# A block joins the deferred blocks, and the adapter's products take operands in high and low parts

## What is computed

```python
x = x + _L0_cond_ref(x, L0_cond_W1, L0_cond_b1, L0_cond_v, itok_B_0_2)
x = x + _L1_cond_ref(x, condB_zX[:, None], condB_zY[:, None], condB_zR[:, None], 1, 1)
x = x + _L2_cond_ref(x, itok_B_0_6, L2_cond_down_w, ..., L2_cond_ln_g, L2_cond_ln_b)
x = x + _L3_cond_ref(x, L3_cond_tau_ctx, condB_tauraws, L3_cond_Wg, ..., L3_cond_Wout, ...)

# L0: softmax-weighted sums over positions, p is 2048 x 2048 with a prefix, suffix or leave-one-out mask
pooled = jnp.einsum('bjl,bld->bjd', p, hidden) / cnt[..., None]
# L1: neighbours in the channel direction (x) and in the position direction (y), reflected at the ends
du_dt = zX[:, :, None] * lap_x + zY[:, :, None] * lap_y + zR[:, :, None] * y * (1.0 - y)
# L2: the adapter, 512 -> 128 -> 512, then a layer norm
z = jax.nn.relu(jnp.einsum('bsh,bhk->bsk', hidden, Wd) + bd)
y = hidden + jnp.einsum('bsk,bkh->bsh', z, Wu) + bu
# L3: exponential averages over positions, a gate from [x, ctx], two traces, soma, gate, output
ctx = causal_ema(x, tau_ctx)
wg = jax.nn.sigmoid(jnp.einsum('btc,ec->bte', jnp.concatenate([x, ctx], axis=-1), Wg) + bg)
```

## Time and profile before

| | us |
|---|---|
| median of 3 runs (lowest, highest) | 701.6 (700.96, 702.64) |
| the profiled execution, its own time | 702.7 |
| its span in the trace | 700.7 |
| TensorE, VectorE, ScalarE, GpSimd busy | 666.1, 526.5, 363.3, 174.2 |

### The profile page before, as it was taken

The page is one execution under the profiler, slowest core; times in us unless marked ns, Lnnn a source line. Parts: engine busy times, 40 slices in busy tenths (PEclk is TensorE's granted clock), DMA queues, the critical chain, the costliest instruction groups (busy, mean ns, idle before and its releaser), DMA issues.

```text
span 700.7 us, 8057 instructions
## 1 busy us (share of the span) xinstructions
PE 666.1 (95%) x2792; PEld 484.8 (69%) x2792; DVE 526.5 (75%) x747; ACT 363.3 (52%) x745; POOL 174.2 (25%) x259
## 2 busy tenths in 40 slices
PE   4969988989999999999999999999999999999996
PEld 1535444468577868786878687868786878687875
DVE  2676789847996888589868986887689649864955
ACT  0143366582675366536653566456635653565245
POOL 5003440110044214411451235123512210111001
PEclk9989999999999999999999999999999999999998
DMA  7996998999522661465147524742465230022001
GB/s 201 326 335 222 258 203 201 359 263 322 106 36 74 150 101 29 102 135 97 30 117 129 87 35 120 131 77 39 127 93 88 38 83 1 0 48 74 0 1 60
DMA packets 51670, 85.77 MB, mean 122 GB/s; under 512 B 8480, under 2 KB 10528, under 8 KB 51630
## 3 DMA queue, kind: packets, MB, share of 16 engines
q0 software_dynamic: 16896, 33.56, 30.1%
q1 hardware_dynamic: 31230, 51.69, 20.6%
q10 hardware_dynamic: 3504, 0.01, 0.3%
HBM read 63.22 MB, written 22.04 MB: 122 GB/s over the span
## 4 chain that ended last, share of the span: by engine, by line
PE 79%; DVE 9%; ACT 4%; DMA 4%; SPq 2%; issue 1%; POOLq 0%; ACTq 0%; POOL 0%; DVEq 0%
PE bank L1130 20%; PE bank L1129 20%; PE bank L1131 20%; PE bank L1184 3%; PE bank L1174 3%; PE bank L1125 3%; PE bank L1030 3%; DMA beside_scratch<-xts 2%; PE bank L1164 2%; PE bank L1193 2%; DMA xts<-in_xT 1%; SPq L410 1%; DVE xb L1513 1%; DVE x2b L1519 1%; PE bank L1224 1%
## 5 line engine op out<-in xcount | busy, mean ns | idle before, releaser
L1668 DVE TENSOR_TENSOR_SCAN tr<-alpha,carry,tr 128x512 f32<-128x512 f32 x48 | 58.8, 1267 | 0.0
L1129 PE MATMUL bank<-th,wg_l 128*128 128x512 f32 x128 | 52.0, 406 | 0.0
L1129 PE MATMUL bank<-xh,wg_l 128*128 128x512 f32 x128 | 51.9, 406 | 0.0
L1130 PE MATMUL bank<-tl,wg_h 128*128 128x512 f32 x128 | 50.5, 395 | 0.0
L1130 PE MATMUL bank<-xl,wg_h 128*128 128x512 f32 x128 | 50.5, 395 | 0.0
L1131 PE MATMUL bank<-th,wg_h 128*128 128x512 f32 x128 | 50.2, 392 | 0.0
L1131 PE MATMUL bank<-xh,wg_h 128*128 128x512 f32 x128 | 50.2, 392 | 0.0
L840 ACT ACTIVATE carry<-tr 128x2 f32<-128x2 f32 x32 | 6.6, 205 | 80.4 <-DVE tr L1668 80.3
L624 POOL TENSOR_TENSOR rs_a<-ss_a,consts 128x1 f32<-128x1 f32 x32 | 14.3, 447 | 118.7 <-ACT junk L788 118.1
L1125 PE MATMUL bank<-xb,probT 128*128 128x512 f32 x64 | 36.4, 652 | 5.5 <-DVE xb L1513 5.4
L1655 DVE SCALAR_TENSOR_TENSOR wgb<-wgb,soma 128x512 f32<-128x512 f32 x32 | 22.2, 692 | 25.4 <-ACT wgb L834 25.4
(11 more groups left out here) (264 smaller groups left out, 1995.3 us busy)
## 6 DMA issues: line engine op xcount, KB each, us to landing
x2b<-beside_scratch POOLq DMA_DIRECT2D x12, 1024.0 KB, 9.2
xr<-rows_scratch POOLq DMA_DIRECT2D x10, 1024.0 KB, 10.6
xb<-in_x SPq DMA_DIRECT2D x8, 1024.0 KB, 14.2
result<-xr SPq DMA_DIRECT2D x7, 1024.0 KB, 4.2
x2b<-rows_scratch POOLq DMA_DIRECT2D x6, 1024.0 KB, 9.5
x_scratch<-xb SPq DMA_DIRECT2D x5, 1024.0 KB, 10.5
beside_scratch<-xts SPq DMA_DIRECT2D x5, 1024.0 KB, 11.5
late_y<-x_scratch SPq DMA_DIRECT2D x20, 256.0 KB, 2.9
```

The costliest lines, as they stand in the source:

```text
L1129: pe.matmul(acc, wl, xh_, start=start, stop=False)
L1130: pe.matmul(acc, wh, xl_, start=False, stop=False)
L1668: ve.tensor_tensor_scan(t[:, d], alpha[:, 1 + d:2 + d].broadcast_to([P, GN]), t[:, d], 0.0 if first else carry[:, k, 1 + d:2 + d], ALU.mul ...
```

## The change

1. `HEAD_BLOCKS` is 2. Block 2 leaves `mix_local`, `channels`, `by_local` and `stencil` of the first stage. Instead SyncE copies it within SBUF (`keep_x1`), and its four tiles are worked on as deferred tiles around the start of the last stage: tiles 0 and 1 beside `x3_lo(0)`, tiles 2 and 3 inside group 0. `add_before(2)` and `add_after(2)` move to the end of group 0.
2. A deferred block is loaded in one DMA of 1 MB into its own buffer `x2_of(q)`. `late_mix` reads that buffer and writes the new single buffer `late_mixed`.
3. From block 1 on, `down` and `up` go through `split3`. ScalarE writes the high parts (`x2_evict` into fp32r, a second `relu` pass, `adapter_hi` in groups 0 and 3), VectorE the low parts (`x2_lo`, four passes; `z_low`, one; `adapter_lo` in groups 0 and 3). `x2_lo` uses `junk`, `junk_o`, `late_mixed` and `late_side` as its four buffers, `z_h` is in `late_side`.
4. In VectorE's list `trace_lo(g, k)` stands one place later, `late_stencil` of tile 3 ahead of `logits(g, 0)`, and tile 2 is handled ahead of `out_apply` 2, no longer 3.
5. The adapter's weights for batch 1 are loaded in group 3, into the same buffers as batch 0's.

```diff
-HEAD_BLOCKS = 3
+HEAD_BLOCKS = 2
...
+        x2h, x2l = wide_r[:], [t[:] for t in (junk_r, junk_o_r, late_mixed_r, late_side_r)]
+        z_h, z_l = late_side_r[:], nar_r[:]
...
+                    def keep_x1(q):
+                        sp.wait_ge(x1_done, GT * (q + 1))
+                        sp.wait_ge(beside_out[0][0], 32)
+                        sp.dma_start(x2_of(q), x1_of(q)).then_inc(late_in, 16)
+
+                    def load_late(q):
+                        sp.wait_ge(x1_out[q], 16)
+                        if q == HEAD_BLOCKS + 1:
+                            beside_landed(sp, 1, 3)
                         else:
-                            sp.wait_ge(late_v, n)
-                            sp.wait_ge(late_chan, 3 * n)
-                        sp.wait_ge(x1_out[q], 16)
-                        sp.dma_start(late_y[:], x1_rows(q)[:, c]).then_inc(late_in, 16)
+                            sp.wait_ge(x3_done, GT * (q - 1))
+                        sp.dma_start(x2_of(q), x1_rows(q)).then_inc(late_in, 16)
...
                     def late_mix(q, c):
                         n, b = late_tile(q, c), q // NG
-                        act.wait_ge(late_in, 16 * (n + 1))
-                        if q == HEAD_BLOCKS:
-                            beside_landed(act, 1, 1)
+                        act.wait_ge(late_in, 16 * (q - 1))
+                        if n:
+                            act.wait_ge(late_v, n)
                         else:
-                            act.wait_ge(x3_done, GT * (q - 1))
-                        act.activation(x2_of(q)[:, c], late_y[:], ACT.Identity, ...
+                            act.wait_ge(pool_mm, B * NT)
+                        if c == 0 and q > FIRST_LATE:
+                            act.wait_ge(down_mm, q - 1)
+                        act.activation(late_mixed[:], x2_of(q)[:, c], ACT.Identity, ...
...
+                        if q:
+                            act.activation(z_h, bank[DOWN(q)][:], ACT.Relu, ...)\
+                               .then_inc(z_act, 1)
...
                     def down(q):
...
+                        pe.wait_ge(aw_lo, 2 * (q // NG + 1))
+                        for k in ks:
+                            pe.wait_ge(x2T_lo, KE * (q - 1) + k + 1)
+                            last = split3(bank[DOWN(q)][:], dw_h[:, k], dw_l[:, k], x2h[:, k], x2l[k],
+                                          k == 0, k == KE - 1)
+                        last.then_inc(down_mm, 1)
+
+                    def up(q):
+                        pe.wait_ge(z_lo, q)
+                        for c in range(GT):
+                            split3(bank[UP(q)[c]][:], z_h[:, chunk(c)], z_l[:, chunk(c)], uw_h[:], uw_l[:],
+                                   True, True).then_inc(up_mm, 1)
...
+                    def x2_lo(q):
+                        for k in ks:
+                            ve.wait_ge(x2T_ev, KE * q + k + 1)
+                            ve.scalar_tensor_tensor(x2l[k], bank[X2T(q)[k]][:], up_cols[:, q // NG, k:k + 1],
+                                                    f32(x2h[:, k]), ALU.add, ALU.subtract).then_inc(x2T_lo, 1)
+
+                    def z_low(q):
+                        ve.wait_ge(z_act, 2 * q + 1)
+                        ve.tensor_tensor(z_l, z[:], f32(z_h), ALU.subtract).then_inc(z_lo, 1)
...
                         if g == 0 and k == 0:
-                            beside_landed(ve, 1, 3)
+                            beside_landed(ve, 1, 2)
...
                         logits(g, 1)
                         blend_traces(g, 0)
                         traces(g, 1)
-                        trace_lo(g, 0)
+                        if g == 0:
+                            late_by_local(2, 3)
+                            late_stencil(2, 3)
                         logits(g, 2)
                         blend_traces(g, 1)
+                        trace_lo(g, 0)
                         traces(g, 2)
+                        logits(g, 3)
+                        if g == 0 or g == NG - 1:
+                            adapter_lo((g + 1) // NG)
+                        blend_traces(g, 2)
                         trace_lo(g, 1)
-                        logits(g, 3)
-                        blend_traces(g, 2)
+                        if adapted:
+                            x2_lo(g + 1)
                         traces(g, 3)
                         trace_lo(g, 2)
+                        if adapted:
+                            z_low(g + 1)
                         blend_traces(g, 3)
```

More of the change, by code:

```diff
@@ L968, in _ @@
                         mod_affine(g)
+                        if g == 0:
+                            late_mix(2, 2)
                         keep_traces(g, 0)
@@ L972, in _ @@
                         trace_hi(g, 0)
+                        if g == 0:
+                            late_mix(2, 3)
                         keep_traces(g, 1)
@@ L1011, in _ @@
                         for c in range(GT):
-                            if late and c == 3:
+                            if late and c == 2:
                                 late_mix(g + 3, 2)
```

151 lines of the change are left out of this document (91 added, 60 removed).

## The result

| | before | changed |
|---|---|---|
| median (lowest, highest) of 4 runs each, us | 701.56 (700.96, 702.64) | 696.2 (694.93, 696.51) |
| ratio of the two, 95% interval | | 0.9919 (0.9901 to 0.9936) |
| the profiled execution, its own time | 702.7 | 696.12 |
| its span | 700.7 | 694.3 |

Faster, by 6.6 us profile against profile (forecast 6.7) and by 5.4 us median against median, which is 0.8%. The forecast of the median was 694.9 with a range of 690 to 699; it is 696.2. In a later set of runs the changed kernel had 696.29 us (696.12 to 697.15, 5 runs) and a ratio of 0.9899 (0.9881 to 0.9917). Two executions at a far lower granted clock (842.5 us at 0.75, of the kernel before, and 1063.5 us at 0.58, of `best`) are left out of all ratios.

The account below looks back on a forecast made before the run. TensorE was taken to bound groups 1 to 6, with VectorE barely in time. First stage and group 0 (-0.7 us) plus the loop (-6.0) took 702.7 to 696.0; the median, 1.1 lower, was forecast at 694.9, range 690 to 699.

Parts of the forecast that it names:

- What bounds: TensorE bounds groups 1 to 6, 69.6 us each; VectorE, busy 75% of the span, is the one to watch.
- 1, Products: `down` and `up`: twelve fp32r products take 2.78 us for 3.43, saving 1.3 us in each of groups 0 to 6.
- 2, VectorE in time: Groups 1 to 6, F being the start of `front(g)`: `up` waits some 0.1 us for `z_low`; 6.0 us gained altogether.
- The cause of the early trace: ScalarE's 3.20 us wait for the last tile's DMA goes, so the first trace moves from F + 14.8 to 13.2.
- 3, The loop's moves at nothing: In the loop, the 1 MB loads, the moved `add_after(2)` and ScalarE's extra passes were costed at nothing.
- 4, First stage: Without block 2's passes, `x2_transposes(0)` starts at 109 us: 3.9 us gained, between 0 and 5.0.
- 5, Group 0: VectorE's list up to `wt_l` grows by 2.4 us net; two `late_mix` passes ahead of `n1_gelu` add 0.8.
- The sum: First stage and group 0 give -0.7 us, the loop -6.0: -6.7 us in all.
- Shared reads: Rival: GpSimd's adds moved into group 0 slow VectorE passes by 2.1 us more, 697.0 us; chance 0.10.
- The slower rival: `late_mix` of tile 3 holds `mod_tanh`, so the traces start no earlier: 1.3 us slower, 702.9 us; chance 0.11.
- The faster rival, 690.0: Group 0 doesn't give the first stage's gain back, or `z_low` is earlier than forecast: 690.0 us; chance 0.10.
- The late load of 1 MB: Rival: the load holds `x3_evict` and so `front`, four groups losing 7 us each: 28 us, 723 us; chance 0.04.

Follow-up runs that it names:

- `best`: Changed kernel with high and low parts only from block 2 on, `z_low` ahead of `trace_lo` of chunk 2, and `mod_tanh` in two halves: 689.14 us.
- Experiments 3 and 4: Edits to the changed kernel: a useless ScalarE pass ahead of `mod_tanh`, 703.76 us; VectorE's list shortened in three separate ways, 693.8, 693.5 and 693.79 us.
- experiment 8: The run of `best`, 689.14 us, ratio 0.9794, beside the changed kernel again, 696.29 us.
- experiment 2: Changed kernel with tile 3's own load put back, 696.4 us; then with tile 2 in its old place too, 697.05 us.
- experiment 7: Kernel before, with most of block 2's own VectorE and GpSimd work in the first stage left out: 698.07 us, ratio 0.9915.
- experiment 1: Changed kernel with item 3 undone, so `down` and `up` take plain fp32 operands in every group: 695.9 us, ratio 0.9895.
- experiment 6: Changed kernel with GpSimd's add of channel neighbours of every deferred tile replaced by a fill with zeros: 694.8 us, ratio 0.9882.
- experiment 3: Changed kernel with a useless ScalarE copy of about 1.5 us ahead of `mod_tanh` in groups 1 to 6: 703.76 us, ratio 1.0009.

## Why the prediction was right, and where its sum was not

- **What bounds.** Right: TensorE in groups 1 to 6, VectorE as the engine to watch. Experiments 3 and 4 show the link in both directions, `z_low` to `up`, to within 0.1 us.
- **1, Products.** The price held: 12 products take 2.80 us (forecast 2.78), and the full gain is 1.2 us in a group (experiment 8) for a forecast of 1.3. The 3.43 x 3/4 = 2.57 that went with the four passes of "FP8 and Floating Point Precision" in the Trainium skill is too low: the trace has 2.80 for the twelve products in fp32r, 0.233 us each, so its count doesn't give the ratio of the times here.
- **2, VectorE in time.** The first trace (F + 13.2) and `z_low` (F + 41.8 forecast, 41.72 measured) were right. The term that was off is the due time of `up`: I put 41.7, it is 41.56. I had taken the start of `down(4)`, 391.54, from the chain, where a piece begins when the record before it ends. The timeline has it at 391.37, F + 35.99, and two sets of twelve products, 2.80 and 2.78 us, lead from there to 41.57. `up` is 0.2 us late in groups 1, 2, 5 and 6, not 0.1, and each of those costs 0.3: these groups give 0.9 and not 1.2. Group 4 gives 1.2: it begins a batch, where the scans have no carried value and are shorter (two take 2.33 us for 2.45), so the last trace starts 0.55 earlier. Group 3 loses 0.3. Measured -4.54 for a forecast of -6.0. The row of the timeline before, for `down(4)`:

```profile
391.37 3.60 PE L1174 MATMUL bank<-wide,dw 128*128 128x512 f32 x8
```

- **The cause of the early trace** was half right. I named the last load's wait of 3.20 us. That wait put back costs nothing (experiment 2); by the traces the wait for tile 1's load ahead of `out_moments` was the one that told, which no run tests by itself. ScalarE waited for two of the four loads of a block, not for all four. Both waits end with item 2, so the number came out, for the right item and by the wrong link.
- **3, The loop's moves at nothing.** Held: the loads of 1 MB landed in 5.6 us (median), no `late_mix` was late, and `add_after(2)` was in time.
- **4, First stage.** -3.9 forecast, -3.81 at F(0), in part by luck: `x2_transposes(0)` gained 4.27, and 0.46 were lost to a pass of the first deferred tile ahead of `x3_lo`, a term that I hadn't. That block 2's passes held the stage is shown by experiment 7.
- **5, Group 0.** VectorE's +2.4 held (2.26, and 2.40 for the group). The 0.8 us for two `late_mix` passes ahead of `n1_gelu` is the failed term: the first trace stands at F + 15.41 and stood at 15.25. So F(1) came 1.4 us earlier and not 0.7. The first wait at `down(1)` is 1.65 us, not the 2 to 3 that I had named as a sign.
- **The sum.** Two errors of opposite sign, 1.5 us in the loop and 0.7 ahead of it, and 0.45 that I hadn't seen behind F(7) leave -6.4 against -6.7. In group 7, where the adapter has no part, the last trace starts at F + 33.46 and not 34.40 (item 4: `trace_lo` fills the gate's waits) and `output(7)` waits 0.9 for 1.25 us. The median is 1.3 us above its forecast (696.2 for 694.9) because I took 1.1 off for the profiled execution of the kernel before, the slowest of its four, and that of the changed kernel stands at its median: chance.
- **What the sum hid.** I set down 6.0 us as the products' gain and their passes in group 0 in another term. Put together, my own terms make item 3 worth 6.0 - 4.5 = 1.5 us; it is 0.25 (experiment 1). TensorE's 1.3 us "not seen in this group" was right, but the question whether the high and low parts should be used there at all wasn't asked.
- **The rivals.** Shared reads: out (experiment 6). The row behind it was true; the adds that moved stand where it costs nothing, and one that both kernels have costs 0.8 us in group 0. The Trainium skill, "SBUF — State Buffer" (Who interferes with whom), says that the conflict is with GpSimd instructions that read SBUF and not with those that only write it; the trace agrees, with 2.13 us beside the add and 1.48 beside the fill. The time of groups 1 to 6 doesn't follow from it. The slower rival was right in mechanism and nearly in price (experiment 3) and failed on its condition: no `late_mix` held `mod_tanh` in the changed kernel. The faster rival, 690.0, failed on both of its conditions: group 0 took 2.40 us back, and `z_low` ended where I had it. The late load of 1 MB: out.
